# A third PSUM bank for the attention scores, a later place for the P·V matmuls, and the output projection's eviction on VectorE

## The reference

```python
xn = _layernorm(x)
x = x + attn(xn) + ffn(xn)
# attn
q = rope(rms_norm(xn @ Wq.T));  k = rope(rms_norm(xn @ Wk.T));  v = xn @ Wv.T
Rq, Rk = xn @ Wrq.T, xn @ Wrk.T             # 12 heads of rank 32
bias = einsum('bhsr,bhtr->bhst', Rq, Rk)    # heads 0-3: (bias + bias.T) / 2; heads 12-15: no bias
scores = q @ k.T / sqrt(128) + bias * graph_scale      # causal mask
out = softmax(scores) @ v @ Wo.T
# ffn
fp16(gelu(xn @ W0.T + b0)) @ W1.T + b1      # 2048 -> 8192 -> 2048
```

## Time and profile before

| | us |
|---|---|
| median of the runs (2 runs, 5541.15 to 5592.08) | 5566.61 |
| the profiled execution, its own time | 5367.02 |
| its span, slowest core (core 1) | 5365.4 |
| spans of the 8 cores | 5317.9 to 5365.4 |
| feed-forward part (from 3304 to the end) | 2061 |
| PE busy, all of the span | 3812.1 (71%) |
| ACT busy | 939.2 (18%) |
| DVE busy | 705.6 (13%) |
| POOL busy | 453.0 (8%) |

### The profile page before, as it was taken

The page is one execution under the profiler, slowest core; times in us unless marked ns, Lnnn a source line. Parts: engine busy times, 40 slices in busy tenths (PEclk is TensorE's granted clock), DMA queues, the critical chain, the costliest instruction groups (busy, mean ns, idle before and its releaser), DMA issues.

```text
span 5365.4 us, 41375 instructions; the slowest of 8 cores (5317.9 to 5365.4 us)
## 1 busy us (share of the span) xinstructions
PE 3812.1 (71%) x14112; PEld 1372.8 (26%) x14112; DVE 705.6 (13%) x1165; ACT 939.2 (18%) x1395; POOL 453.0 (8%) x548
## 2 busy tenths in 40 slices
PE   1367654457664865546775568998998899889987
PEld 0123111112111311112111123333343333333333
DVE  5422122111121111210101100000000000000000
ACT  1110022202222222231222342100010011001100
POOL 0000012211212011111011010000000000000000
PEclk9868566667565856767656779999999999999999
DMA  2201334253334333344123313445445544554454
GB/s 89 86 24 57 94 127 138 94 173 109 128 118 143 109 114 139 125 150 162 64 97 125 102 48 122 141 157 162 149 141 163 162 146 134 170 162 136 144 161 146
DMA packets 176448, 672.10 MB, mean 125 GB/s; under 512 B 22002, under 2 KB 30322, under 8 KB 152178
## 3 DMA queue, kind: packets, MB, share of 16 engines
q1 hardware_dynamic: 108146, 400.98, 23.8%
q10 hardware_dynamic: 36864, 159.40, 9.1%
q0 software_dynamic: 31232, 109.07, 5.0%
HBM read 560.32 MB, written 109.05 MB: 125 GB/s over the span
## 4 chain that ended last, share of the span: by engine, by line
PE 47%; DMA 33%; issue 5%; ACT 4%; DVE 4%; POOL 3%; POOLq 2%; ACTq 2%; DVEq 0%; SPq 0%
DMA wcbb<-wbf 17%; PE ps L738 14%; DMA wcbf<-w 8%; PE ps L765 8%; PE ps L492 5%; PE ps L295 3%; PE ps L632 3%; PE ps L576 3%; DMA wcbf<-wv 3%; PE ps L587 3%; PE ps L639 3%; POOLq L131 2%; POOL ar L621 2%; PE ps L697 2%; DMA wbf<-wcbb 2%
## 5 line engine op out<-in xcount | busy, mean ns | idle before, releaser
L765 PE MATMUL ps<-ar,wcbb 128*128 128x512 bf16 x4096 | 918.8, 380 | 147.5 <-DMA wcbb<-wbf 137.8
L738 PE MATMUL ps<-xnT,wcbb 128*128 128x512 bf16 x4096 | 916.9, 381 | 68.8 <-DMA wcbb<-wbf 50.3
L576 PE MATMUL ps<-ar 128*128 128x512 bf16 x640 | 332.7, 543 | 444.4 <-ACTq L131 444.3
L607 ACT ACTIVATE ar<-ps,cstS 128x512 bf16<-128x512 f32 x640 | 424.2, 686 | 852.4 <-DMA wcbf<-w 347.1
L765 PEld LDWEIGHTS ps<-ar,wcbb 128*128 128x128 bf16 x4096 | 385.9, 98 | 680.4 <-issue 254.3
L738 PEld LDWEIGHTS ps<-xnT,wcbb 128*128 128x128 bf16 x4096 | 387.7, 98 | 598.0 <-issue 174.2
L632 PE MATMUL ps<-ar 128*128 128x512 bf16 x640 | 344.2, 538 | 230.5 <-POOLq L131 230.4
L746 ACT ACTIVATE ar<-ps,b0S 128x512 bf16<-128x512 f32 x256 | 175.9, 687 | 1596.1 <-PE ps L738 1596.1
L492 PE MATMUL ps<-xnT,wcbb 128*128 128x512 bf16 x1024 | 266.2, 420 | 132.3 <-DMA wcbb<-wbf 74.1
L621 POOL TENSOR_TENSOR ar<-ar,maskS 128x512 bf16<-128x512 bf16 x256 | 288.9, 1148 | 786.8 <-ACTq L131 759.8
L639 PE MATMUL ps<-ar,onesmS 128*128 128x512 bf16 x640 | 351.2, 549 | 0.0
(11 more groups left out here) (70 smaller groups left out, 1535.3 us busy)
## 6 DMA issues: line engine op xcount, KB each, us to landing
wcbb<-wbf SPq DMA_DIRECT2D x608, 512.0 KB
wcbf<-w ACTq DMA_DIRECT2D x128, 1024.0 KB, 5.1
wbf<-wcbb POOLq DMA_DIRECT2D x160, 512.0 KB, 4.5
wcbf<-x SPq DMA_DIRECT2D x16, 1024.0 KB
wcbf<-wv SPq DMA_DIRECT2D x64, 256.0 KB
wcbf<-wq SPq DMA_DIRECT2D x16, 1024.0 KB
wcbf<-wo SPq DMA_DIRECT2D x16, 1024.0 KB
xtb<-xT ACTq DMA_DIRECT2D x64, 256.0 KB, 4.1
```

The lines of the kernel that those rows point to most:

```text
L576: return e.matmul(bank[:, :], ar[:, KT_O + g * S + tt * 128: KT_O + g * S + (tt + 1) * 128], ar[:, QT_O + hh * 512:QT_O + hh * 512 + 512], ...
L607: e.activation(ar[:, PB_O + slot * 512:PB_O + (slot + 1) * 512], bank[:, :], AF.Exp, bias=cstS[:, C_NEGC:C_NEGC + 1])
L738: return e.matmul(bank[:, :], wcbb[:, slot * 2048 + ec * 128: slot * 2048 + (ec + 1) * 128], xnT[:, ec * S + sc * 512: ec * S + sc * 512 + ...
L765: return e.matmul(bank[:, :], wcbb[:, slot * 2048 + i * 128: slot * 2048 + (i + 1) * 128], ar[:, HACT_O + ncb * 512:HACT_O + (ncb + 1) * 512],
```

## The change

It has three parts.

1. The score groups go round three banks, `ps[0]`, `ps[1]` and `ps[3]`, by `tt % 3`, in place of two. After the exponentials of a pair only the banks that this pair has used are noted as free. The rotation of the next Q projection, which also uses `ps[3]`, waits for the last exponential that read it; the first use of `ps[3]` by the scores waits for all that DVE had to do up to the last rotation.
2. The AV pairs of the tiles up to `tt - 3` (not `tt - 2`) are called after the odd tile, and before each exponential those up to `tt - 4`, so that the SBUF slot of that exponential is free.
3. The copy of an output projection block out of PSUM goes from ACT to DVE (an `activation` with Copy becomes a `tensor_copy`), and the waits go with it.

```diff
-    sc_ps_free = [(sDV, a0_end_dv), (sDV, a0_end_dv)]
+    sc_ps_free = [(sDV, a0_end_dv), (sDV, a0_end_dv), (sDV, a0_end_dv)]
+    ps3_exp = [0]
...
-                def mk_rope(hh=hh, h=h, bank=bank, par=par, rs_o=rs_o, v_r3=v_r3):
+                def mk_rope(hh=hh, h=h, bank=bank, par=par, rs_o=rs_o, v_r3=v_r3,
+                            ps3w=ps3_exp[0]):
...
-                        v_rot = pe(f_rot, (sDV, v_qraw), inc=True)
+                        v_rot = pe(f_rot, (sDV, v_qraw), (sAC, ps3w), inc=True)
...
             while rope_q:
                 rope_q.pop(0)()
+            sc_ps_free[2] = (sDV, sDV.n)
...
-                    par = tt % 2
-                    bank = ps[par]
+                    par = tt % 3
+                    bank = ps[[0, 1, 3][par]]
...
                             v_sc = pe(f_b2m, inc=True)
+                    while av_called[0] <= tt - 4:
+                        av_q[av_called[0]]()
+                        av_called[0] += 1
                     slot = tt % 4
...
-                    sc_ps_free[0] = (sAC, v_exp)
-                    sc_ps_free[1] = (sAC, v_exp)
+                    for t2_, _s in pend_t:
+                        sc_ps_free[t2_ % 3] = (sAC, v_exp)
+                        if t2_ % 3 == 2:
+                            ps3_exp[0] = v_exp
...
-                    while av_called[0] <= tt - 2:
+                    while av_called[0] <= tt - 3:
                         av_q[av_called[0]]()
                         av_called[0] += 1
...
             def f_ev(e, bank=bank, y1slot=y1slot):
-                e.activation(ar[:, y1slot:y1slot + 512], bank[:, :], AF.Copy)
-            op("scalar", f_ev, (sPE, v_mm), y1st_free[eoc % 2])
-            v_ev = flush("scalar")
-            qps_free[par] = (sAC, v_ev)
+                e.tensor_copy(ar[:, y1slot:y1slot + 512], bank[:, :])
+            op("vector", f_ev, (sPE, v_mm), y1st_free[eoc % 2])
+            v_ev = flush("vector")
+            qps_free[par] = (sDV, v_ev)
             v_sp = dma("gpsimd", d_y1sp[eoc * 128:(eoc + 1) * 128, sc * 512:sc * 512 + 512],
-                       ar[:, y1slot:y1slot + 512], (sAC, v_ev))
+                       ar[:, y1slot:y1slot + 512], (sDV, v_ev))
```

## The result

| | before | changed |
|---|---|---|
| median of all runs, us | 5480.24 (10 runs, 5368.46 to 5592.08) | 5432.22 (11 runs, 5322.9 to 5545.71) |
| profiled execution, us | 5367.02 | 5341.47 |
| ratio to before | | 0.9893, 95% interval 0.9854 to 0.9931 |
| the same in a second comparison (below) | | 0.9933, 95% interval 0.9910 to 0.9957 |

The change makes the kernel about 0.7 to 1.1% faster, some 36 to 57 us. The forecast was −43 us. The forecast time, 5523, was set on the median of the two runs then known, 5566.61; with eight more runs that median is 5480.24.

The account below looks back on a forecast made before the run. Large waits were put down to ACT's spill-load transfers once per head, with PE otherwise mostly the bound. Savings 13.5 + 18 + 3 + 5.5 + 3.4 = 43 us, taken off the two-run median, gave 5523 us; range 5435 to 5605.

Parts of the forecast that it names:

- What bounds the kernel: Attention heads: the large waits come once per head, from ACT standing at spill loads (11.67 us), not from the banks.
- The start of a head: Third score group runs while ACT stands at the spill loads; 9 heads of 3 matmuls save 1.5 us each, 13.5.
- The 2-matmul heads: Stages 2 to 4: 21 heads behind spills save 0.85 us each, midway between 1.05 and 0.7, together 18 us.
- the later AV pairs: Tail of each head: costs nothing, since the score group comes earlier by just the AV pair; otherwise 41 us.
- The half-beginnings: Six head starts after the Q projection in stages 2 to 4, without the long stall: 0.5 us each, 3 saved.
- The steady pairs: Inside heads: nothing saved at the lower clock; 1-matmul pair 1.91 to 1.70 us, saving 5.5 (stage 4) and 3.4 (stage 3).
- The eviction: Output projection copy on DVE: 0 us, hidden, in stage 1 by POOL's two stores; uncovered, 29 + 6 us.
- A: Rival: the score waits are about the banks, and all 444.3 us go, giving 5122 us; chance 0.02.
- B: Rival: the 2-matmul heads reach the upper clock at once after the stall, 78 us more saved, 5446; chance 0.09.
- C: Rival: the 2-matmul heads never leave the lower clock, costing 82 us, giving 5606; chance 0.09.
- the prediction's own sign of being wrong: Forecast is wrong if PEclk in windows of the 2-matmul heads differs from 0.63 by more than 0.1.
- D: Rival: the tail is not neutral or eats the gain at the head's start, 43 − 41, 5565 us; chance 0.10.

Follow-up runs that it names:

- a second comparison: The whole changed kernel run again without any edit, beside the kernel before on one chip: ratio 0.9933 (0.9910 to 0.9957), −36 us.
- two groups ahead: Five PSUM banks for the score groups in place of three, against the kernel with the third bank alone: 5286.74 us in the profiled execution.

## Why the prediction was right or wrong, point by point

**What bounds the kernel: right.** That the 444.3 us are mainly ACT at its transfers was argued from two views; moving the loads to another queue shows it (444 to 109).

**The start of a head: right in the 3-matmul heads.** 13.5 us forecast, 13.9 and 15.2 measured in the two profiles, 12.4 with the bank alone, and 25.0 with two groups ahead. From the first to the fourth exponential alone it is 13.5 (41.2 to 27.7). In stage 4 heads 1 to 3 took 50.8, 50.1 and 50.3 us in the mean of the cores; they now take 48.8, 48.8 and 49.0.

**The 2-matmul heads: the step that failed.** 18 us forecast, 11.1 and 13.4 measured. The term was not mis-sized at the bank: the start of these heads gives 22.6 us, 1.08 per head, which is the full 1.05 of a score group at the lower clock. What failed is that the later AV pairs and the steady pairs were costed at nothing there. The prediction compared kinds of matmul at the lower clock and took the upper clock to come "at an unchanged time". With the later AV pairs it comes later: between the fourth and the last exponential it holds for 69 to 70 us, not 92 to 100, and this middle takes 275 us in place of 257 to 263. With the bank alone it is 89 us and 255.7. The tail gives 5 us back. The difference between the bank alone and the whole change is 8 to 11 us in these heads; the later AV pairs without the bank cost them 50. Why the clock rises later in this order is not shown: at the lower clock PE's pair is 3.85 us in both.

**The half-beginnings: head 0 right, head 8 wrong in sign.** −3 us forecast for both in stages 2 to 4. From its first score group on, head 0 takes 3.3 and 3.1 us less in the three stages together than before, and as much less with the bank alone. Head 8 takes 4.7 and 5.2 us more; the bank alone gives −0.7, the AV pairs alone +9.7. It is the same step that failed: head 8 is a 2-matmul head, and between its fourth and last exponentials the upper clock holds for 6 and 7 us, where it was 19, and 17 with the eviction alone.

**The steady pairs: right but for one.** 4.70 and 3.85 us at the lower clock, unchanged; 1.76 in the 1-matmul heads, 1.70 forecast. The 1-matmul heads gave 9.0 and 9.2 us, 8.9 forecast, with −6.4 to −6.9 in stage 4 (5.5 forecast) and −3.2 in stage 3 (3.4). The 2-matmul pair at the upper clock, which the prediction read as "again without a wait", did wait 0.15 us for ACT and went from 2.29 to 2.18.

**The eviction: right.** Nothing was forecast, with 35 us as the upper bound; alone it measures 1.0015 (0.9991 to 1.0039), and leaving it out changes nothing. The cover that was named, POOL's two stores, is in the rows of stage 1. On DVE the copy takes 692 ns, as the row of the other copy said:

```profile
L716 DVE CAST ar<-ps 128x512 bf16<-128x512 f32 x64 | 44.3, 692 | 270.1 <-PE ps L705 167.4 <-DMA y1sp<-ar 95.8 <-DMA wbf<-wcbb 6.9
```

**The rivals.** A (−444) is out. B, a rise of the clock: it did not come in the 2-matmul heads. C, a fall: in part it did, with some 22 to 31 of the 92 to 100 us lost in the middle of these heads and 10 to 13 more in head 8; it went further in the AV pairs alone, and also with five banks. The cause C gave, the group that lies ahead of the stall, is not it: the bank alone has that group too and keeps 89 us. The windows of whole heads, 0.63 before and after, did not show it, so the prediction's own sign of being wrong, a PEclk off by 0.1, was too coarse. The clock also rose where I had given it none: the 3-matmul heads have 16 to 17 us at the upper level (2 before, 2 with the bank alone, 16 with the AV pairs alone), 7 of them ahead of the first exponential, 9 to 10 behind the last, and none between. D, a tail that eats the gain: no; the tails of the 3-matmul and 2-matmul heads are 3 and 5 us shorter in the whole change.

**The sum, and the time.** −43 us forecast; −36 by the second ratio, −57 by the first, −28 up to the last head in the first pair of profiles. The side was right, and so was the size, −0.8% against −0.7 to −1.1%. The terms as the two profiles measure them are a little below the forecast: 13.9 + 11.1 − 5.0 (head 7 to head 8) + 9.0 = 29 and 15.2 + 13.4 − 4.0 + 9.2 = 34, with some 3 more from head 0. That one ratio lies on the far side of 43 is no support for the sum. What put the measured time outside the range was the last step, from the sum to a time: "I take 43 off it" from a median of two runs, and the remark that this median carries "some 25 us of its own". The two were the highest and the third highest of the ten now known, and with ten runs the median is 86 us lower. 5480 − 43 = 5437 would have been 5 us from the measured 5432. The range was drawn from the bounds of the change and half of a scatter read from two runs; the shift between the medians was twice the sum.

## What to carry to other kernels

A wait that stands on an engine's compute instruction may belong to that engine's transfers: an in-order queue that issues a load behind a wait for the one before holds back everything behind it, and two lines that move the issue to another queue gave some 4% where a third PSUM bank gave 1%. A change of several parts should be costed and tried part by part: here one part gained 56 us, one cost some 20 of them again, and one did nothing. When an order is shifted, write down the whole round trip of each engine in the new order, in every place and at both clocks, and not only at the head's end. And a mean clock over a stretch in which the engine also stands does not tell what clock its work ran at: take windows over the working part alone.

## What the runs showed of the hardware that was not expected

In the 3-matmul heads of stage 4 PE works for some 33 us on end, from the first exponential to the last, and the clock stays at 0.50, its lower level of 1.2 GHz. With the loads on SP's queue it still does in the kernel before, though there the stand at a head's start is short (0.95 us in head 1; heads 2 and 3 of stage 4, the window of that profile):

```profile
2482.18:2562.97 80.79, 75.72 (x161) 14.79 (x160) 8.74 (x8) 24.62 (x36) 13.81 (x14) 0.50 0.34 117
```

PE's row is busy for 75.72 of 80.79 us there. The Trainium skill (TensorE: Matmul & The Clock Gate, Part 1) says that activity releases the throttle; in this stretch the trace does not agree, as far as a busy row is activity. What these heads have and the 1-matmul heads (0.83) have not are matmuls of 32 rows, 4 of the 10 matmuls of a pair of tiles; in the 2-matmul heads (0.63) it is 2 of 8. Whether they have to do with it was not tried.

The upper-level pair of the 2-matmul heads went from 2.29 to 2.18 us, though no view lists a wait there, before or after. The timeline of before (head 6 of stage 4) has one just at the length below which a view leaves it out:

```profile
2890.72 1.33 ACT L607 ACTIVATE ar<-ps,cstS 128x512 bf16<-128x512 f32 x2 [0.96 <-PE ps L587]
...
2891.86 0.38 PE L639 MATMUL ps<-ar,onesmS 128*128 128x512 bf16 x1
2892.22 0.38 PE L576 MATMUL ps<-ar 128*128 128x512 bf16 x1
```

L576 starts 0.36 us behind L639 and 0.17 behind the end of the exponentials (2892.05), which is the time that ACT's signal takes in the earlier trace rows too. In all 195 such pairs of stages 3 and 4 the median is the same, and L576 follows the exponentials by 0.165 to 0.168 us in nine of ten. In the changed kernel and with the bank alone the same step on PE takes 0.22 us. So at the upper clock ACT's round trip bounded the 2-matmul pair too, by 0.15 us, and the third bank takes that away.
